# A recommender tower on one core: one more field looked up on TensorE, in ten slices

## What is computed

```python
e = jnp.stack([tbl_0[ids[:, 0]], ..., tbl_31[ids[:, 31]]], axis=1)   # 2048 x 32 x 16
z = jnp.sum(e[:, row, :] * e[:, col, :], axis=2)                     # 496 pairs
h = jnp.concatenate([z, dense_ctx], axis=1)                          # 512
h = jnp.maximum(h @ W_top1 + b_top1, 0.0)                            # 512
h = jnp.maximum(h @ W_top2 + b_top2, 0.0)                            # 256
y = h @ W_top3
```

## Time and profile before

| | us |
|---|---|
| median of three runs | 390.6 (388.05 to 390.77) |
| the profiled execution | 392.31 |
| its span, first to last instruction | 390.5 |
| TensorE busy | 301.6 (77%) |
| VectorE busy | 248.0 (63%) |
| GpSimd busy | 227.9 (58%) |
| ScalarE busy | 145.0 (37%) |
| TensorE's mean granted clock | 0.921 |

### The profile page before, as it was taken

The page is one execution under the profiler, slowest core; times in us unless marked ns, Lnnn a source line. Parts: engine busy times, 40 slices in busy tenths (PEclk is TensorE's granted clock), DMA queues, the critical chain, the costliest instruction groups (busy, mean ns, idle before and its releaser), DMA issues.

```text
span 390.5 us, 7439 instructions
## 1 busy us (share of the span) xinstructions
PE 301.6 (77%) x2748; PEld 278.9 (71%) x2748; DVE 248.0 (63%) x326; ACT 145.0 (37%) x311; POOL 227.9 (58%) x250
## 2 busy tenths in 40 slices
PE   1658697999777967977796797879679786978377
PEld 1348696888776857977785797768579776877366
DVE  6798769565956567394647739464673946556541
ACT  3982443434442424344242434424243441113012
POOL 6446655566656656665665666566566656657700
PEclk9988899899998999889899988989998898999759
DMA  6770020202020200102030110202012000000000
GB/s 140 207 236 5 8 64 6 65 6 64 8 63 5 64 6 15 53 6 63 5 64 6 24 44 6 63 6 64 6 17 51 6 6 5 7 8 6 7 3 1
DMA packets 19036, 14.51 MB, mean 37 GB/s; under 512 B 9727, under 2 KB 16461, under 8 KB 19022
## 3 DMA queue, kind: packets, MB, share of 16 engines
q1 hardware_dynamic: 10284, 11.69, 9.9%
q0 software_dynamic: 7680, 1.98, 6.5%
q10 hardware_dynamic: 1058, 0.66, 0.6%
HBM read 14.24 MB, written 0.08 MB: 37 GB/s over the span
## 4 chain that ended last, share of the span: by engine, by line
POOL 24%; PE 24%; issue 20%; DMA 11%; DVE 7%; another core or an unknown queue 6%; ACT 6%; SPq 1%; POOLq 0%; DVEq 0%; ACTq 0%
POOL emb L367 24%; DMA emb<-tbl,idx 10%; PE bank L663 7%; PE bank L683 6%; PE bank L645 5%; DVE emb L470 2%; PE bank L642 2%; ACT distance L844 2%; PE bank L780 1%; DVE prod L480 1%; DVE prod L489 1%; PE bank L692 1%; PE bank L699 1%; DVE mask L438 1%
## 5 line engine op out<-in xcount | busy, mean ns | idle before, releaser
L367 POOL DMA_INDIRECT emb<-tbl,idx x240 | 226.7, 945 | 141.8 <-DMA emb<-tbl,idx 80.1
L489 DVE TENSOR_TENSOR prod<-emb,bank 128x1904 f32<-128x1904 f32 (+5 forms) x51 | 94.5, 1854 | 99.3 <-DMA emb<-tbl,idx 97.3
L663 PE MATMUL bank<-ident,prod 128*128 128x128 f32 x768 | 101.9, 286 | 11.6 <-issue 4.5
L663 PEld LDWEIGHTS bank<-ident,prod 128*128 128x128 f32 x768 | 94.1, 197 | 14.3 <-issue 5.7
L683 PE MATMUL bank<-zT,w_sb 128*128 128x128 f32 x480 | 73.4, 303 | 17.7 <-ACT zT L882 16.5
L645 PE MATMUL bank<-parts,onehot 125*128 125x160 bf16 (+1 forms) x816 | 84.8, 239 | 1.8 <-issue 1.7
L683 PEld LDWEIGHTS bank<-zT,w_sb 128*128 128x128 f32 x480 | 65.9, 213 | 21.5 <-issue 19.8
L645 PEld LDWEIGHTS bank<-parts,onehot 125*128 125x128 bf16 x816 | 68.0, 104 | 1.2 <-issue 0.7
L642 PE MATMUL bank<-far_ten,named_ten 100*128 100x160 bf16 x160 | 40.9, 256 | 36.1 <-issue 26.6
L470 DVE TENSOR_REDUCE emb<-bank 128x480 f32 (+5 forms) x96 | 52.6, 583 | 10.3 <-remote 4.3
L875 ACT COPY bank<-emb 128x112 f32 (+3 forms) x32 | 7.8, 243 | 107.7 <-issue 68.4
(11 more groups left out here) (71 smaller groups left out, 137.4 us busy)
## 6 DMA issues: line engine op xcount, KB each, us to landing
gids<-small_ids_f SPq DMA_DIRECT2D x16, 544.0 KB
emb<-tbl,idx POOLq DMA_INDIRECT x240
w_sb<-w SPq DMA_DIRECT2D x1, 1024.0 KB
w_sb<-w SPq DMA_DIRECT2D x1, 512.0 KB
tab<-tbl SPq DMA_DIRECT2D x7, 56.0 KB
tab<-tbl SPq DMA_DIRECT2D x5, 70.0 KB
tab<-tbl ACTq DMA_DIRECT2D x5, 70.0 KB
z_last<-dense SPq DMA_DIRECT2D x16, 8.0 KB
```

What stands on the lines that cost most here:

```text
L367: nc.gpsimd.indirect_dma_start(emb[:, t, at:at + D], None, tables[f], bass.IndirectOffsetOnAxis(ap=idx[:, t, f:f + 1], axis=0)).then_inc(d ...
L489: return nc.vector.tensor_tensor(prod[:, at * D:(at + n * a) * D].rearrange("p (j i d) -> p j i d", j=n, d=D), strided(emb_at(t, PLACES[g] ...
L663: mm = nc.tensor.matmul(bank[:, Z_BANK + place, c * P:(c + 1) * P], v[:, d, :], ident[:], start=(d == 0), stop=(d == D - 1), is_transpose= ...
```

## The change

Field 26 has 12500 rows, that is ten slices of 1250, each as large as a small table. From tile 3 on (`FIRST_SLICED = 3`) it is looked up on TensorE instead of gathered. The ids less 1250 times the slice's number, in units of rows, are broadcast as `sids`; ScalarE makes a one-hot for each of ten slices (nothing is hot in the nine that don't hold the id); ten slices x three parts are 30 matmuls behind one of the kind of L642, into 160 free columns of the bank of round 3; VectorE's `pick_sliced` takes the maximum. In tiles 0 to 2 the field is gathered as before. GpSimd issues 227 gathers.

With it come:

- **Rows of gathers.** GpSimd waits after each fifth gather of a tile and after its last one: rows of 5, 5 and 4 where the tile has 14. Group 0 has field 26 as its first.
- **Strided maxima.** All tables now lie as (field, candidate, column). ScalarE's first copy is packed, and `pick` reads at a step of 16 elements. The numbers of the masks' rows grow by one field.
- **Sums.** `TURN_SUMS` is 2. Even tiles keep chunk 2 on TensorE, odd ones have it summed by VectorE (`sum_pairs` over 150 sums instead of 22 ahead of the last group) and turned.
- **TensorE's order.** After the turn the lookups of rounds 2 and 3 with the slices, then the sum of chunk 0, and layer 1 behind it; layers 2 and 3 stand at different places in even and odd windows.
- **The table of field 26** is loaded after the weights into `tab`, and split into three parts in windows 0 and 1: TensorE subtracts the parts (`first_rest_of_slices`, `second_rest_of_slices`), ScalarE copies (`slice_first_of`, `slice_second_of`, `slice_third_of`).
- **ScalarE** takes the distances in two pieces with a copy between them, `apart` after group 0's copy and `onehot_slices` after group 1's. SyncE's `load_sids` waits until `apart` of the tile before is done.

```diff
+SLICED = 26
+SLICES = VOCABS[SLICED] // (ROWS * SLOTS)
+SLICED_ROUND, SLICED_COL = 3, 320
+FIRST_SLICED = 3
+SLICE_ROUNDS = [(0, 3), (3, 3), (6, 3), (9, 1)]
...
-TURN_SUMS = 3
+TURN_SUMS = 2
...
+            def load_sids(t):
+                sp.dma_start(sids[:], slices[t * SLICES * P:(t + 1) * SLICES * P].rearrange("(o x) -> o x", o=1)
+                             .to_broadcast([P, SLICES * P])).then_inc(sids_loaded, 16)
...
+            sp.wait_ge(tab_copied, 2 * len(ROUNDS))
+            rows_of_slices = tables[SLICED].rearrange("(s p c) d -> p s (c d)", p=ROWS, c=SLOTS)
+            table = tab[:, 0:SLICES * SLOTS * D].rearrange("p (s x) -> p s x", s=SLICES)
+            sp.dma_start(table[0:EVEN, :, :], rows_of_slices[0:EVEN, :, :]).then_inc(table_loaded, 16)
+            sp.dma_start(table[EVEN:ROWS, :, :], rows_of_slices[EVEN:ROWS, :, :]).then_inc(table_loaded, 16)
...
                     load_gids(t + 1)
+                    if t + 1 >= FIRST_SLICED:
+                        if t + 1 > FIRST_SLICED:
+                            sp.wait_ge(slices_apart, sliced_before(t + 1))
+                        load_sids(t + 1)
...
                     for i in range(n):
                         f = FIELDS[GROUP_AT[g] + i]
+                        if f == SLICED and t >= FIRST_SLICED:
+                            continue
...
-                        place = GROUP_AT[g] + i - S
-                        if t < LAST_TILE and place % RUN == RUN - 1:
-                            pool.wait_ge(done, 16 * (t // 2 * n + i + 1))
+                        gathered += 1
+                        in_group += 1
+                        if t < LAST_TILE and (gathered % RUN == 0 or f == FIELDS[F - 1]):
+                            before = first_group_landed(t % 2, t // 2, t - 2 < FIRST_SLICED) if g == 0 else t // 2 * n
+                            pool.wait_ge(done, 16 * (before + in_group))
...
-                    emb_at(t, SMALL_PLACE + first, n).rearrange("p a x -> p (a x)"),
-                    bank[:, from_bank, 0:width_of(r)].rearrange("p (x c) -> p x c", c=CANDS[first]),
+                    emb_at(t, SMALL_PLACE + first, n).rearrange("p a (f d) -> p (a f) d", d=D),
+                    bank[:, from_bank, 0:width_of(r)].rearrange("p (f c d) -> p f d c", c=CANDS[first], d=D),
...
+            def pick_sliced(t):
+                at = SLICED_COL
+                nc.vector.tensor_reduce(
+                    emb_at(t, PLACES[0], 1).rearrange("p a x -> p (a x)"),
+                    bank[:, LOOK_BANK + SLICED_ROUND % 2, at:at + SLOTS * D].rearrange("p (c d) -> p d c", d=D),
+                    AX.X, ALU.max)
...
-                sum_pairs(t, place, SUM_AT, PAIR_AT[5])
+                sum_pairs(t, place, SUM_AT + (1 - place) * P, PAIR_AT[5])
...
+                if apart and r == SLICED_ROUND:
+                    look = bank[:, to_bank, SLICED_COL:SLICED_COL + SLOTS * D]
+                    at = TEN_FIELDS.index(SLICED) * SLOTS * D
+                    nc.tensor.matmul(look, named_ten[0:ten_rows, bass.ts(t, P)],
+                                     far_ten[0:ten_rows, at:at + SLOTS * D], start=True, stop=False)
+                    for k in range(SLICES):
+                        for i in range(PARTS):
+                            mm = nc.tensor.matmul(look, sliced[:, place, k, :], slice_parts[:, i, k, :],
+                                                  start=False, stop=(k == SLICES - 1 and i == PARTS - 1))
...
+                if place == 1:
+                    sum_chunk(t - 1, 1 - place, 2, GROUP1_STEP)
+                elif before > 1:
+                    layer2(t - 2)
                 if before > 0:
-                    sum_chunk(t - 1, 1 - place, 2, GROUP1_STEP)
                     turn_sums(t - 1, 1 - place, loads)
-                if before > 1:
-                    layer2(t - 2)
-                if before > 0:
-                    layer1(t - 1, 1 - place, 0)
-                if before > 1:
-                    layer3(t - 2)
                 if look:
-                    look_up_rounds(t + 1, 1 - place, (2, 3))
+                    look_up_rounds(t + 1, 1 - place, (2, 3), apart)
...
+            def apart(t, place, k):
+                act.wait_ge(sids_loaded, 16 * (k + 1))
+                act.wait_ge(looked, rounds_done(t - 2, SLICED_ROUND))
+                nc.scalar.activation(
+                    sliced[:, place, :, :].rearrange("p s (j n) -> p s j n", n=SUB),
+                    sids[0:ROWS, :].rearrange("p (j s n) -> p s j n", s=SLICES, n=SUB),
+                    ACT.Abs, bias=minus_row[0:ROWS, :]).then_inc(slices_apart, 1)
```

280 lines of the change are left out of this document (207 added, 73 removed).

## The result

The changed kernel takes 402.05 us (median of 4 runs, 401.11 to 402.70) against 390.29 us for the kernel before (388.05 to 390.77): a ratio of 1.031, 95% interval 1.026 to 1.036. The forecast was 377.0 us with a range of 373 to 388. It is slower by 3%, where faster by 3.5% was forecast.

What follows compares the result with a forecast made beforehand. GpSimd's unbroken string of gathers was taken as the bound: -16.2 us for gathers, +2.0 start, +0.7 broadcasts, -13.5 in all. With the end unchanged, 392.3 became 378.8, less 1.7 to the median: 377 us, range 373 to 388.

Steps and rivals of the forecast that it cites:

- GpSimd's sum: GpSimd's path: 13 gathers fewer save 16.2 us, start costs 2.0 and broadcasts 0.7, net -13.5 us; tile 21.7 us.
- start and broadcasts together: GpSimd's rows: 2.0 us for loading field 26's table at the start, 0.7 us for slice-id broadcasts meeting rows.
- The sizes on VectorE: VectorE's tile: 14.4 us plus 1.07 for odd tiles' longer reduction and 0.32 for the slice's maximum, 15.8 of 21.7.
- The strided maxima: VectorE's maxima read at a stride: 0 us extra taken, up to 2.8 us a tile at twice the cost.
- The rival that needed it: VectorE and TensorE take turns as the bound: maxima at twice the cost, 21.9 to 22.5 us a tile, 380 to 387; chance 0.18.
- The end is the same code, 390.5 - 369.59 = 20.9 us, and stays: After GpSimd's last gather: the remaining time was taken as unchanged at 20.9 us.
- the warning: Last tiles: if VectorE no longer waits for rows there, the end belongs to another engine than said; no size given.
- 2.0 us remain: TensorE in the loop: 19.7 us of work in a new tile of 21.7 us, leaving 2.0 us idle.
- two rivals: Late TensorE completions: 3.2 us where VectorE and TensorE take turns (0.18), 1.3 us where TensorE becomes the bound (0.08).
- made up at 2 us a tile: After windows 0 and 1: their 6 to 8 us delay is recovered at 21.7 - 19.7 = 2 us a tile before the end.
- TensorE becomes the bound, and it gets slower: TensorE between turn and lookups of rounds 2 and 3: 3.1 us plus 1.3 late, 24.1 us a tile, 407; chance 0.08.
- decides from 22.96: That TensorE rival's threshold: its tile sets the time only from 22.96 us, the kernel before's tile.

Runs made afterwards that it cites:

- b4: The kernel before, with GpSimd also waiting after the fifth and tenth gather of the last tile: 385.43 us, 0.988 of the kernel before.
- e3: The changed kernel, with GpSimd also waiting after the fifth and tenth gather of the last tile: 391.50 us, 1.002 of the kernel before.
- a3: The changed kernel with a small GpSimd memset in place of each gather: 341.42 us in one run, kernel before 420.53 on that chip.
- b3: The kernel before with a GpSimd memset in place of each of its 240 gathers: 295.16 us in one run, against 390.69 with gathers.
- f1: The changed kernel with one GpSimd wait a tile, all 14 gathers in one row: 340.07 us in one run, kernel before 392.96.
- a1: The changed kernel without the slices' 30 matmuls a tile on TensorE: 396.88 us in one run, kernel before 420.53 on that chip.

## Why the prediction was wrong

**GpSimd's sum was right in kind.** The last gather moved from 369.59 to 360.19, forecast 356.1. GpSimd waits for its own transfers alone, never for products, and its tile is 21.7 us outside the rows that meet a broadcast. The 4.1 us are those rows: gaps between two gathers above 2.9 us have 13.4 us over the usual 2.6 (8 gaps), against 6.7 us before (4). The prediction had 2.7 for start and broadcasts together; 6.7 came, 2.8 of it in the two rows of the start (2.0 forecast) and 3.9 in the later ones (0.7 forecast). The kernel before had three such later rows, at 49.6, 73.8 and 90.3, where the prediction counted one. Here is one, the broadcast of the groups and the row that it meets, with 3.96 us where 1.6 is usual:

```profile
97.38 0.43 SPq L340 DMA_DIRECT2D gids<-small_ids_f  x1
```

```profile
102.78 0.94 POOL L431 DMA_INDIRECT emb<-tbl,idx  x1 [3.96 <-DMA emb<-tbl,idx]
```

**The sizes on VectorE were right.** By shape (count, busy us, mean ns, idle before):

```profile
L542 DVE TENSOR_REDUCE emb<-bank 128x480 f32 x24 | 14.5, 647 | 0.0
L542 DVE TENSOR_REDUCE emb<-bank 128x320 f32 x24 | 11.5, 481 | 0.4 <-remote 0.4
...
L596 DVE TENSOR_REDUCE z_last<-prod 128x150 f32<-128x2400 f32 x7 | 18.6, 2653 | 0.8
L549 DVE TENSOR_REDUCE emb<-bank 128x160 f32 x12 | 3.9, 324 | 26.9 <-PE bank L739 16.0 <-remote 10.9
L972 ACT COPY bank<-tab 125x480 f32<-125x480 f32 x2 | 1.1, 566 | 4.2 <-DMA tab<-tbl 4.2
```

The strided maxima take 647 and 481 ns, the packed ones took 648 and 484: nothing, the value taken. The slice's maximum is 324 ns (0.32 forecast), the long reduction 2.13 us more (2.1 forecast), ScalarE's packed copy 566 (558). The Trainium skill (Advanced Engine Details and Errata, Memory Cachelines) has a cost for SBUF where each access goes to another line, and for PSUM it speaks of matmuls; the prediction carried it over to VectorE. For VectorE's reads of PSUM no such cost shows here, and the measurement decides. The rival that needed it had the wrong ground.

**The step that failed is the end.** "The end is the same code, 390.5 - 369.59 = 20.9 us, and stays" took for granted that GpSimd sets the end. Even in the kernel before about 10 of the 20.9 us (b4) were late completions in the last, unbroken row of gathers. Now 39.1 us follow the last gather, since TensorE and VectorE are a window behind it: 18.2 of the 22.3 us that the forecast missed. The prediction gave the warning itself, that the end belongs to another engine if VectorE no longer waits for rows in the last tiles, but no number to it. Two waits on GpSimd take 9.9 us of it back (e3, chip E).

**"2.0 us remain" failed in the loop.** TensorE's load was near enough: 18.7 us a tile without gathers against 19.7 said. But late completions stood only in two rivals, at 3.2 us in one and 1.3 in the other. The tile is 22.3 to 22.8 us on A and C, 3.6 to 4.1 over 18.7 and 0.6 to 1.1 over the 21.7 forecast. Most of VectorE's part of it (25.4 of 35.5 us) is at one place, its maxima of round 4 (128x512 elements), behind a look-up that is recorded as done at 224.7 and seen at 227.69, when a row of gathers has landed and GpSimd goes on at 228.07:

```profile
224.37 0.33 PE L729 MATMUL bank<-parts,onehot 125*128 125x128 bf16 x3
...
227.69 1.15 DVE L542 TENSOR_REDUCE emb<-bank 128x512 f32 x2 [4.67 <-remote]
...
228.07 0.94 POOL L431 DMA_INDIRECT emb<-tbl,idx  x1 [1.66 <-DMA emb<-tbl,idx]
```

The prediction had seen such a pair (2.78 us before ScalarE's copy) and let VectorE's waits for rows absorb it. They did, while GpSimd was behind; with them gone each late completion counts.

**The start was not made up.** Windows 0 and 1 end 10.1 us later (products of tile 2 at 74.0 for 63.9), 6 to 8 were forecast. The larger miss is "made up at 2 us a tile": 8.7 us are still there at tile 3 and 12.5 at tile 14 (345.3 for 332.8). Nothing was left over to make it up with.

**The rivals.** "TensorE becomes the bound, and it gets slower" had 0.08 and gave 407 us; 402 came. It named late completions, and as the place the maxima of rounds 0 and 1 behind the small products, where TensorE waits for VectorE 11.2 us in the whole span; it priced the tile at 24.1 us for 22.8 and had nothing of the last window. That 407 is near 402 is partly luck. That it "decides from 22.96" was wrong: what counts is GpSimd's new 21.7.

## What to carry to other kernels

A wait that is hidden today behind the engine that binds is a price for tomorrow. Before taking work from the binding engine, sum the waits of the second chain with no help from the first: leave the first engine's work out in one run, as a3 and b3 do, and look for waits that no instruction ends. Read the tail behind the binding engine's last instruction as waits and work of its own, not as a constant, and try where a pause in a long string of gathers may make the whole faster. A gain or loss of 3% that hangs on such waits may turn with the chip, so measure on more than one.

## What the runs showed of the hardware

- On chips A, B, C and E, in every run with gathers, while GpSimd's gathers are in flight, TensorE's results reach other engines up to 12.6 us late. In that longest case its matmuls also come 0.7 or 1.4 us apart (a chunk of 16 in 10 us for 1.97); in a short one they do not (15 transposes in 2.07 us from 224.53). It ends when a row has landed. Two pauses of GpSimd in 14 gathers cut the longest wait from 12.4 to 4.7 us. What holds them is not in the trace.
- With it, 56 to 63% of the gathers' semaphore updates are missing from the trace, and about 1% at most where it is absent. Which of the two makes the other, or what makes both, is open.
- The same program shows this on chips B and E and not on D (421, 391 and 378 us for one kernel). Chips D and F never showed it in six kernels that have gathers.
- Where it is absent, 227 gathers beside TensorE and VectorE cost them nothing (f1 338.3 us of span against a3 339.5 without a gather).
- Chip B runs the kernel before at 420.5 us, the others at 390 to 396. a3 on chip B and f1 on chip F agree within 1.4 us, so chip B is as fast as F where no completion is late. a1 at 396.9 us shows that TensorE's load weighs there; why it weighs more than on E was not looked for.
